# A fused GNN and expert kernel: the flag of ordered edges read ahead of the first barrier, five normalized tiles behind the build, and the second group's scatters in two rows

## What is computed

```python
x = x + L0_gnn(_layernorm(x), src, dst, edge_weight, ...)   # two rounds of (x + A x) W, layer norm, gelu; then Wp
x = x + L0_ffn(_layernorm(x), ...)                          # shared MLP + 4 experts, gates' best 2
x = x + L1_gnn(_layernorm(x), edge_index, ...)              # two GCN convolutions, symmetric norm
x = x + L1_ffn(_layernorm(x), ...)                          # router, best 2 of 8 experts per token:
#   out = tokens
#   for e in range(8):
#       out = out + combine[:, e:e+1] * (gelu(tokens @ w1[e] + b1[e]) @ w2[e] + b2[e])
```

## Time and profile before

| | us |
|---|---|
| median of 3 runs | 1837.85 (1836.99 to 1849.55) |
| the profiled execution's own time | 1837.97 |
| its span in the trace | 1836.2 |
| PE busy | 1710.8 (93%) |
| DVE busy | 944.4 (51%) |
| ACT busy | 570.0 (31%) |
| POOL busy | 186.5 (10%) |

### The profile page before, as it was taken

One profiled execution on the slowest core, in us unless ns is written; L12 is line 12 of the kernel. 1 busy time (PEld: TensorE's weight loads), 2 busy tenths in 40 slices (PEclk: granted clock), 3 DMA queues, 4 the chain that ended last, 5 costly groups with the idle time before them and its releaser, 6 DMA issues.

```text
span 1836.2 us, 30852 instructions
## 1 busy us (share of the span) xinstructions
PE 1710.8 (93%) x10162; PEld 1367.8 (74%) x10163; DVE 944.4 (51%) x1594; ACT 570.0 (31%) x854; POOL 186.5 (10%) x260
## 2 busy tenths in 40 slices
PE   6999999888879999999999999999999999998985
PEld 4998988887766777787777777766677777777774
DVE  7999999999861310111143443553213243346436
ACT  3135677888870100000011111344200000014442
POOL 4000000000000100000000000000000000153763
PEclk9999999999999999999999999999999999999998
DMA  4103344445569445454434336700073443443375
GB/s 97 1 34 132 147 171 197 201 189 215 222 249 347 129 140 158 130 173 143 133 119 124 119 116 161 196 1 0 18 258 110 137 118 118 152 138 96 110 221 182
DMA packets 136919, 261.73 MB, mean 143 GB/s; under 512 B 22236, under 2 KB 74735, under 8 KB 136606
## 3 DMA queue, kind: packets, MB, share of 16 engines
q1 hardware_dynamic: 116824, 237.02, 39.6%
q0 software_dynamic: 5808, 14.70, 2.2%
q10 hardware_dynamic: 14230, 9.29, 1.7%
HBM read 161.13 MB, written 108.09 MB: 147 GB/s over the span
## 4 chain that ended last, share of the span: by engine, by line
issue 55%; PE 31%; ACT 5%; DVE 5%; DMA 1%; POOL 1%; DVEq 1%; ACTq 1%; POOLq 0%; SPq 0%
PE ps L2065 13%; PE ps L2096 6%; PE ps L2066 4%; ACT wide L868 3%; PE ps L2300 2%; ACT ps L816 2%; PE ps L2316 2%; DVE act_c L1371 1%; PE ps L2113 1%; PE ps L1968 1%; PE ps L2308 1%; PE ps L2292 1%; POOL routed_tokens L1192 0%; ACTq L857 0%; PE ps L2125 0%
## 5 line engine op out<-in xcount | busy, mean ns | idle before, releaser
L2096 PE MATMUL ps<-wide 128*128 128x320 f32 (+1 forms) x2000 | 536.6, 429 | 0.0
L2096 PEld LDWEIGHTS ps<-wide 128*128 128x128 f32 x2000 | 380.5, 191 | 142.7 <-issue 1.6
L2065 PE MATMUL ps<-early,act_c 128*128 128x200 bf16 x2400 | 296.4, 252 | 42.9 <-ACT ps L816 21.0
L2096 PE MATMUL ps<-wide,act_a 128*128 128x320 f32 (+1 forms) x1000 | 264.4, 426 | 2.3 <-DMA wide<-weight_matrix 2.1
L2065 PEld LDWEIGHTS ps<-early,act_c 128*128 128x128 bf16 x2400 | 221.2, 98 | 57.2 <-issue 56.1
L2096 PEld LDWEIGHTS ps<-wide,act_a 128*128 128x128 f32 x1000 | 189.8, 190 | 75.5 <-DMA wide<-weight_matrix 2.4
L868 ACT COPY wide<-ps 128x832 f32<-128x832 f32 x200 | 169.9, 849 | 123.1 <-PE ps L2066 121.8
L816 ACT ACTIVATE ps<-wide 128x832 f32 (+1 forms) x200 | 173.4, 868 | 41.1 <-ACT wide L868 33.7
L1371 DVE TENSOR_TENSOR act_c<-act_a,pair_tab 128x3072 bf16<-128x3072 bf16 x98 | 170.1, 1770 | 15.0 <-PE ps L2066 14.9
L1499 DVE TENSOR_TENSOR wide<-ps,rows 128x1280 f32<-128x1280 f32 x10 | 14.9, 1492 | 286.2 <-PE ps L2113 286.2
L2065 PE MATMUL ps<-act_a,act_c 128*128 128x200 bf16 x1152 | 140.4, 251 | 12.0 <-ACT ps L816 5.2
(11 more groups left out here) (254 smaller groups left out, 1814.3 us busy)
## 6 DMA issues: line engine op xcount, KB each, us to landing
wide<-weight_matrix SPq DMA_DIRECT2D x90, 800.0 KB, 4.5
wide<-count_matrix SPq DMA_DIRECT2D x45, 800.0 KB, 4.6
weight_matrix<-wide SPq DMA_DIRECT2D x60, 480.0 KB, 2.5
count_matrix<-wide SPq DMA_DIRECT2D x60, 480.0 KB, 2.6
weight_matrix<-wide SPq DMA_DIRECT2D x20, 560.0 KB, 2.7
count_matrix<-wide SPq DMA_DIRECT2D x20, 560.0 KB, 2.7
wide<-weight_matrix SPq DMA_DIRECT2D x20, 400.0 KB, 3.8
routed_tokens<-in_x_dram SPq DMA_DIRECT2D x2, 3072.0 KB, 28.9
```

What stands on the lines that cost most here:

```text
L2065: nc.tensor.matmul(weights, hot_parts[:, slot % PART_SLOTS, part, two, :, k], hot_key[mask_slot][:, mask_two, 0:WCOLS, k], start=False, st ...
L2096: i = nc.tensor.matmul(ps[:, 2 * sub + h, 0:n], features[:, q * QUADS + t, h * P:(h + 1) * P], moving, start=q == 0 and t == 0, stop=q == ...
```

## The change

Three things are changed.

1. The flag's load moves ahead of the first barrier on PE and on ACT. DVE's last step on the flag now counts on `order_steps` (the renamed `chunk_ends`), for which PE and ACT wait before they load it. On PE the bank openings become a function, called inside each of the two branches, so that PE branches first and meets the barrier behind the branch. The two credits (`pair_done`, `onehot_used`) move into the branch that uses them.
2. `norm_input(0)` on DVE, with its wait for `rstd_ready`, moves from ahead of the barrier to behind the build, ahead of `compute_end`.
3. In POOL's loop for the second group the ten scatters of a row follow each other, with one `know_rows` beside every even tile; no replies stand among them. Two replies (`BETWEEN`) are sent between the rows. The loop leaves 15 replies sent and 29 parts known, where it left 23 and 37.

```diff
+BETWEEN = 2
@@ scalar
             keep_weights(2, 5)
+            act.wait_ge(order_steps, 3)
+            disordered = act.value_load(disorder_tab, min_val=0, max_val=1)
             stage_end(act, 1)
@@
             act.wait_ge(banks_opened, 1)
-            disordered = act.value_load(disorder_tab, min_val=0, max_val=1)
@@ gpsimd
                 if n == 0:
                     mark(0)
                 else:
+                    for i in range(BETWEEN):
+                        send_reply(sent)
+                        sent += 1
                     pool.wait_ge(tokens_routed[1], 16 * len(GROUP_TILES[1]))
                     mark(1)
                 for t in GROUP_TILES[1]:
                     route(1, t, n)
-                    if known < FIRST_PART[1]:
+                    if t % 2 == 0:
                         know_rows(known)
                         known += 1
-                    if t % 2 == 0:
-                        send_reply(sent)
-                        sent += 1
@@ vector
-            dve.tensor_copy(disorder_tab, disorder).then_inc(dve_chain, 1)
-            dve.wait_ge(dve_chain, count(1))
+            dve.tensor_copy(disorder_tab, disorder).then_inc(order_steps, 1)
+            dve.wait_ge(order_steps, 3)
             disordered = dve.value_load(disorder_tab, min_val=0, max_val=1)
-            dve.wait_ge(rstd_ready, 1)
-            norm_input(0)
             stage_end(dve, 1)
@@
+            dve.wait_ge(rstd_ready, 1)
+            norm_input(0)
             compute_end(dve, 1)
@@ tensor
-            stage_end(pe, 1)
-            for bank in range(ACCS):
-                i = nc.tensor.matmul(ps[:, bank, 0:PCOLS], ...)
-            i.then_inc(banks_opened, 1)
-
-            pe.sem_inc(pair_done, LEAD)
+            pe.wait_ge(order_steps, 3)
             disordered = pe.value_load(disorder_tab, min_val=0, max_val=1)
-            pe.sem_inc(onehot_used, OH)
+
+            def open_banks():
+                stage_end(pe, 1)
+                for bank in range(ACCS):
+                    i = nc.tensor.matmul(ps[:, bank, 0:PCOLS], ...)
+                i.then_inc(banks_opened, 1)
@@
             with pe.If(disordered > 0):
+                open_banks()
+                pe.sem_inc(onehot_used, OH)
@@
             with pe.If(disordered < 1):
+                open_banks()
+                pe.sem_inc(pair_done, LEAD)
```

More of the change, by code:

```diff
@@ L435, in build_program @@
         windows_taken = sem("windows_taken")
-        chunk_ends = sem("chunk_ends")
+        order_steps = sem("order_steps")
         next_min = sem("next_min")
@@ L1292, in _ @@
             dve.tensor_scalar(low_i, dst_i, 15, 5, ALU.bitwise_and, ALU.logical_shift_left).then_inc(dst_split, 1)
-            dve.tensor_reduce(chunk_min[:, 0:CROWS], d3, AX, ALU.min).then_inc(chunk_ends, 1)
+            dve.tensor_reduce(chunk_min[:, 0:CROWS], d3, AX, ALU.min).then_inc(order_steps, 1)
             dve.wait_ge(windows_taken, 1)
@@ L1300, in _ @@
             dve.wait_ge(next_min, 1)
-            dve.tensor_tensor(unsorted, chunk_max, next_ps, ALU.is_gt).then_inc(chunk_ends, 1)
+            dve.tensor_tensor(unsorted, chunk_max, next_ps, ALU.is_gt).then_inc(order_steps, 1)
             dve.tensor_single_scalar(free_tab, free_tab, 1, op=ALU.logical_shift_right).then_inc(dve_chain, 1)
@@ L1975, in _ @@
             gather(1, [w_n[0]])
-            pe.wait_ge(chunk_ends, 1)
+            pe.wait_ge(order_steps, 1)
             pe.wait_ge(consts_ready, 5)
@@ L1982, in _ @@
             gather(2, key_n[0:2])
-            pe.wait_ge(chunk_ends, 2)
+            pe.wait_ge(order_steps, 2)
             nc.tensor.matmul(unsorted_ps, ones[:, 0:1], unsorted, start=True, stop=True).then_inc(order_summed, 1)
@@ L1993, in _ @@
             gather(5, [w_n[2]])
-            stage_end(pe, 1)
-            for bank in range(ACCS):
-                i = nc.tensor.matmul(ps[:, bank, 0:PCOLS], ones_half[:, :], ones_half[:, 0:1].broadcast_to([P, PCOLS]), start=True, stop=True)
-            i.then_inc(banks_opened, 1)
-            pe.sem_inc(pair_done, LEAD)
-            disordered = pe.value_load(disorder_tab, min_val=0, max_val=1)
-            pe.sem_inc(onehot_used, OH)
+            pe.wait_ge(order_steps, 3)
+            disordered = pe.value_load(disorder_tab, min_val=0, max_val=1)
+            def open_banks():
+                stage_end(pe, 1)
+                for bank in range(ACCS):
+                    i = nc.tensor.matmul(ps[:, bank, 0:PCOLS], ones_half[:, :], ones_half[:, 0:1].broadcast_to([P, PCOLS]), start=True, stop=True)
+                i.then_inc(banks_opened, 1)
             def pair(g, par):
```

## The result

| | before | after |
|---|---|---|
| median | 1842.43 us (20 runs, 1836.99 to 1849.55) | 1834.53 us (20 runs, 1832.87 to 3588.89) |
| the profiled execution's own time | 1837.97 | 1833.34 |
| its span | 1836.2 | 1831.6 |

The ratio of after to before is 0.9967, with a 95% interval of 0.9956 to 0.9977: about 6.1 us faster (4.2 to 8.1). Single executions of two to seven thousand us, here and in the experiments, were disturbed; they are not in the ratios. Three numbers have to be kept apart. Against the forecast of 1829.0 the median is 5.5 us too long. The profiled executions differ by 4.6 us where 9.0 were forecast. And the three runs that the forecast started from had a median of 1837.85, which over 20 runs became 1842.43.

The account below looks back on a forecast made before the run. DVE's masks were taken to pace the build's first half, and late scatters to hold PE at part 37. Gains of 7.86 + 0.85 + 0.28 = 8.99 us took 1837.97 to 1829.0 us; range 1826.5 to 1833.0.

Parts of the forecast that it names:

- The scatters' term: Second group's scatters: rows without replies between end PE's wait for part 37 and the slow restart, gaining 7.86 us.
- (b): Second group's replies: reply 15 lands late behind tile 24's slow scatter, delaying reply 31 by 2.4 us; 1831.4 us, chance 0.05.
- (c): Second group's scatters: back to back they land more slowly, part 37 stays late; half the gain lost, 1832.9 us, chance 0.08.
- (d): Replies behind the rows: SP holds part 53 until reply 36 lands; slower than before, 1841.3 us, chance 0.02.
- The barrier's term: First barrier: opens at 39.7 instead of 40.56, gaining 0.85 us, plus 0.28 us of DVE waiting for PE.
- Rival (a): First barrier: PE comes last, its branch now in front; opens at 41.7, 1.1 us later; 1830.9 us, chance 0.13.
- a gain of 0.85 us for DVE's first mask, and with it for the build: Start of build: a barrier open at 39.7 brings DVE's first mask, and the whole build, 0.85 us earlier.
- the 0.28 us wait at 52.38: DVE's wait for PE in the build's first rounds, forecast to go as PE can start sooner; gain 0.28 us.
- The normalization's cost of nothing: Build's end: 1.71 us of moved DVE work hides in 12.37 us of idle time behind the last mask; cost nothing.
- The middle: First batch-norm sums to the second group's first scatter: forecast difference 0.

Follow-up runs that it names:

- controlled kernels: Experiment kernels with one more register instruction ahead of ACT's pair_done and PE's acc_free waits; unchanged otherwise, the kernel before took 1853.9 us, the kernel after 1842.74 us.
- controls: Kernels before and after with only that register instruction added: before 1853.9 and 1851.41 us; after 1842.74, 1845.41 and, on another chip, 1876.36 us.
- added step: A register maximum with 1, changing no count, ahead of ACT's pair_done and PE's acc_free waits; in the kernel before, ratio 1.0052 and 1.0051.

## Why the prediction was wrong

**The scatters' term was right** in mechanism and size: 7.86 us forecast, 7.73 in the plain traces. Its steps held too. The tenth scatter was put 11.54 us behind the first and came after 11.73; the last was put 29.56 us behind it and came after 30.19; part 37 was down in time. Replies were not late (b), the scatters did not land too late (c), and SP's wait for reply 36 (d) left PE without a wait ahead of part 53: from 1736 to 1800 PE's longest wait is the 0.43 us behind ACT's bias. The controlled kernels give the same part 8.78 us in the trace and 6.3 (3.5 to 9.2) in time.

**The barrier's term failed**, forecast at 0.85 + 0.28 us of gain. Its openings gained more than I gave them: 1.70 us (40.56 to 38.86). Rival (a) came by its condition and not by its price: PE was the last to the barrier, but load and branches took it only 1.4 us (37.35 to 38.74), where I had counted 1.7 us for the load and up to 2.6 for the branch, so the barrier opened earlier and not later. The step that failed is "a gain of 0.85 us for DVE's first mask, and with it for the build". It takes the barrier's opening for the mask's release. In the kernel before, the two were 0.44 us apart, because the credit `pair_done` was given ahead of the branch. The change puts the credit behind the openings and behind the jump, and I listed what stood in front of the barrier on PE and not what stood behind it. I even had the room for a stall of up to 2.6 us from the earlier trace rows, but let it act on the barrier alone. It acted behind it: 2.32 us (1.79 to 2.34 in the three controls of the same kernel) between the last opening and the credit, the mask 1.54 us later than before. The experiments isolate that: the credit moved (mask 3.35 us earlier), the branches swapped (gap gone at the barrier, back at the build's end), the skipped body left out (gap gone at both). The Trainium skill (Runtime: NRT & Kernel Launch, section Instruction fetch mechanics) says that a taken branch to a page that is not held stalls until it is fetched. These runs agree that such a jump stalls, here for 2.3 us, but not on where: eight openings behind the target still ran first. No view shows which instructions PE held.

**From the mask to the build's end** the plain pair loses 1.86 us. 1.54 us of later mask less the 0.28 us wait at 52.38, which is gone as forecast, make 1.26. ACT's tenth copy of a group confirms that: 124.77 before, 125.94 after, 1.17 later. The other 0.6 us come further on, and I can't assign them. In the controls the sign is the other way round: mask 1.13 us later both times, tenth copy 0.84 us earlier and 0.14 later, sums 2.22 and 1.24 us earlier. So what the early loads and the moved normalization do together to the plain build is known from one pair of traces only. In the controlled kernels the pieces are the normalization alone, 2.80 or 1.66 us earlier at the build's end by the control taken, and the early loads, which give back 0.71 to 1.06 of it. A reading that fits is that the added step slows PE, so that the first pair and not the mask paces the start there; it was not tested, and the runs with both loads late and with ACT's load alone early speak against it: they agree in mask and pair and differ by 1.75 us at the sums.

**The normalization's cost of nothing was right** where it went: it lies in DVE's idle time at the build's end. Its removal in front is what the barrier's 0.85 us stood for: up to 1.7 us, halved because I let the early loads on PE and ACT hold the barrier back. They did not: with the loads left behind the barrier, the normalization taken out alone starts the mask at 39.09 where the control has 41.41. (The expectations above that credit the 0.85 us to the early loads misread this term; theirs was only the 0.28.)

**The middle was taken as fixed.** It differs by 1.27 us in the plain pair. Nothing of the change runs there. In twelve profiled executions of the controlled kernels in the three faster sets of runs it runs from 1158.1 to 1173.7 us, for the same kernel 1173.74 and 1158.12. The range of the forecast, 1826.5 to 1833.0, had almost no room for that, nor for a start value from three runs that was 4.6 us under the median of twenty. The steps add up to the traces: 9.0 forecast, less 0.13 at the scatters, 2.99 at the build and 1.27 in the middle are 4.6. The times agree: 9.0 lies outside the measured 4.2 to 8.1 us, and the scatters' 7.73 less the build's 1.86, which is 5.9, inside.

**Best version.** None of the orders at the barrier could be told from the kernel after by its time in more than one set of runs. By the traces, openings and credits ahead of the jump end the build 0.4 to 1.2 us earlier, both loads late 0.7 to 1.1, and ACT's load alone early 2.8 us, this last in one trace. All were compared only with the added step in them, so I would take openings and credits ahead of the jump for their trace and not claim a time.

## What to carry over

When code is moved across a barrier or into a branch, follow each semaphore that the other engines wait for to its new place, and not only the barrier's last arrival; give credits to others ahead of a jump, so that the stall behind it falls on the engine that has slack. A jump's stall can be moved to where it is covered, but swapping the two branches here only shifted it to the other end. And cut the traces at marks into stretches before pricing a difference: a stretch in which nothing changed shows how much one execution strays.

## What the runs showed of the hardware

- A forward jump over PE's branch for unordered edges left PE without an instruction given out for 2.32 us (1.79 to 2.34 in three further traces), though the eight openings behind the target ran at once; from the branch to the credit it is 4.12 us (3.60 to 4.15). With the body left out there was no gap. At the end of the build the jump took 4.03 us from PE's last weight load to its next step, and 2.5 us of the path. One packet of 0.02 MB on the instruction queue q8 goes with it each time.
- TensorE's granted clock fell from 1.00 to 0.50 (2.4 to 1.2 GHz) behind the barrier: in the kernel before in 41 to 42, in the middle of the openings, with PE idle for 3.35 us ahead of them; after the change only in 44 to 45, with PE idle since 40.45. Both first pairs (46.86 and 47.43) ran at 0.50, three matmuls in 0.68 us, and in both the clock rose again in 51 to 52, with PE busy since its first pair. With the branches swapped the pair at 44.73 took 0.44 us.
- One register instruction more ahead of each of the two waits in the build makes the kernel 0.5% slower (1.0052 and 1.0051): the sums start at 555.27 and 554.13 instead of 543.17.
- The same kernel's median (the kernel before) was 1841 us in three sets of runs and 1863 in one, on another chip. In that set of runs the last stretch of the changed kernel takes 25 us more, with a clock of 0.67 in 1736 to 1766.
